# Local attention over six layers: the values product joins a ring of three PSUM banks, the output projection comes in two halves, and the slots are set anew

## The reference

```python
x = x + tanh(g_xattn) * xattn(layernorm(x), ctx)        # 4 x 512 x 128, once, small
h = layernorm(x)
for i in range(6):                                      # DEPTH
    s = shift_tokens(h)                                 # second half of the channels one token later
    q, k, v = split(s @ Wqkv[i])                        # 16 heads of 64
    q, k = l2norm(q) * q_scale[i], l2norm(k) * k_scale[i]
    q, k = rotary(q) * 8, rotary(k)
    # local attention: windows of 32 tokens see themselves and the window before
    p = softmax(mask(q @ k.T))
    h = (p @ v) @ Wo[i] + h
    s = shift_tokens(h)
    xn = (s - mean) / sqrt(var + 1e-5) * ln_g[i] + ln_b[i]
    a, gate = split(xn @ W1[i] + b1[i])                 # 341 each
    h = (a * gelu(gate)) @ W2[i] + b2[i] + h
x = x + tanh(g_ffn) * h
```

## Time and profile before

| | us |
|---|---|
| median of 3 runs (2105.93 to 2115.34) | 2112.6 |
| the profiled execution | 2110.48 |
| its span | 2108.7 |

### The profile page before, as it was taken

The page is one execution under the profiler, slowest core; times in us unless marked ns, Lnnn a source line. Parts: engine busy times, 40 slices in busy tenths (PEclk is TensorE's granted clock), DMA queues, the critical chain, the costliest instruction groups (busy, mean ns, idle before and its releaser), DMA issues.

```text
span 2108.7 us, 47754 instructions
## 1 busy us (share of the span) xinstructions
PE 1841.2 (87%) x17716; PEld 1082.4 (51%) x17716; DVE 1557.8 (74%) x2708; ACT 1314.2 (62%) x2363; POOL 1490.1 (71%) x1200
## 2 busy tenths in 40 slices
PE   6778888999899899889998888988898989989986
PEld 4445555555555555555555555555555555555542
DVE  4588778688678778687787776776877867867862
ACT  2366757657657657576576566575766765765762
POOL 2498678688677777786876776767868767868750
PEclk7699999999999999999999999999999999999998
DMA  3012212122222212222222221222222211221221
GB/s 94 20 52 69 60 50 61 47 59 68 56 59 68 54 49 72 58 64 55 52 57 58 70 63 51 59 53 60 69 53 60 63 49 50 53 61 49 56 54 30
DMA packets 154986, 120.41 MB, mean 57 GB/s; under 512 B 42577, under 2 KB 151173, under 8 KB 154629
## 3 DMA queue, kind: packets, MB, share of 16 engines
q1 hardware_dynamic: 154757, 117.35, 20.9%
HBM read 18.66 MB, written 1.05 MB: 9 GB/s over the span
## 4 chain that ended last, share of the span: by engine, by line
PE 40%; SPq 19%; DVE 18%; DMA 8%; ACT 7%; issue 6%; POOL 2%; DVEq 0%; POOLq 0%; ACTq 0%
SPq L1143 11%; PE ring_bank L456 8%; DMA vw<-vs 8%; PE sc_bank L408 5%; PE ring_bank L502 5%; SPq L1149 4%; PE qk_bank L363 4%; SPq L1146 4%; PE pv_bank L432 4%; PE ring_bank L421 3%; PE ring_bank L374 2%; PE ring_bank L395 2%; PE ring_bank L384 2%; PE ring_bank L445 2%; DVE xnT L921 2%
## 5 line engine op out<-in xcount | busy, mean ns | idle before, releaser
L1016 POOL TENSOR_TENSOR turned<-qkn,tables 128x512 f32<-128x512 f32 x384 | 489.5, 1275 | 462.7 <-DVE qkn L832 378.4
L1023 POOL TENSOR_TENSOR turned<-qkn,tables 128x512 f32<-128x512 f32 x384 | 489.8, 1276 | 0.0
L640 ACT ACTIVATE kB<-ring_bank 64x512 f32<-64x512 f32 x384 | 226.8, 591 | 335.3 <-PE ring_bank L395 333.1
L363 PE MATMUL qk_bank<-wqkv,xT 128*128 128x512 f32 x768 | 364.1, 597 | 0.0
L806 DVE TENSOR_REDUCE ss<-sq 128x16 f32<-128x1024 f32 x192 | 232.2, 1210 | 48.8 <-ACT sq L604 48.5
L878 DVE TENSOR_TENSOR o<-pv_bank,rr 128x512 f32<-128x512 f32 x192 | 132.1, 688 | 180.2 <-ACT oT L677 180.1
L1059 POOL TENSOR_TENSOR turned<-turned 128x512 f32<-128x512 f32 x192 | 251.2, 1308 | 15.1
L1052 POOL TENSOR_TENSOR turned<-turned 128x512 f32<-128x512 f32 x192 | 245.7, 1279 | 15.1
L613 ACT ACTIVATE vs<-ring_bank 128x512 f32<-128x512 f32 x192 | 114.3, 595 | 214.2 <-DMA vw<-vs 191.1
L408 PE MATMUL sc_bank<-kB,qT 128*32 128x128 f32 x6144 | 224.0, 290 | 2.8 <-ACT sc_bank L650 2.8
L604 ACT ACTIVATE sq<-qk_bank 128x1024 f32<-128x1024 f32 x192 | 196.3, 1023 | 42.7 <-PE qk_bank L363 39.6
(11 more groups left out here) (155 smaller groups left out, 3107.6 us busy)
## 6 DMA issues: line engine op xcount, KB each, us to landing
vw<-vs SPq DMA_DIRECT2D x1152, 64.0 KB, 2.0
vw<-vs SPq DMA_DIRECT2D x672, 32.0 KB, 1.9
wqkv<-in_L_ffn_Wqkv_dram SPq DMA_DIRECT2D x20, 384.0 KB, 3.3
wo<-in_L_ffn_Wo_dram SPq DMA_DIRECT2D x20, 128.0 KB, 3.2
w<-in_L_ffn_W_dram SPq DMA_DIRECT2D x6, 341.0 KB, 3.4
wqkv<-in_L_ffn_Wqkv_dram SPq DMA_DIRECT2D x1, 1536.0 KB, 9.8
x<-in_x_dram SPq DMA_DIRECT2D x2, 512.0 KB, 4.0
out_dram<-x SPq DMA_DIRECT2D x4, 256.0 KB, 2.3
```

What stands on the lines that cost most here:

```text
L363: mm = pe.matmul(QK[u % 2][:, i * UW:(i + 1) * UW], tok, wqkv[:, layer % 2, cut:cut + UW], start=True, stop=True)
L1016: return pool.tensor_tensor(heads(turned[:, u % 2, 2 * i, :]), heads(qkn[:, u % 2, i * UW:(i + 1) * UW]), table.unsqueeze(1).to_broadcast( ...
L1023: return pool.tensor_tensor(halves(turned[:, u % 2, 2 * i + 1, :]), halves(qkn[:, u % 2, i * UW:(i + 1) * UW])[:, :, ::-1, :], table.rearr ...
```

## The change

The bank of `attend` becomes the third bank of the ring. `attend` now takes a turn there, and every wait for `pv_mm` and `o_done` becomes one for its turn. `project_out` makes two products of 256 tokens, each after four units, and `add_attention` adds each half. DVE copies the variance with the epsilon added out of PSUM (`add_eps`), ACT's seed and the Newton step then read SBUF, and the square goes to `xnT`. The orders of all loops but POOL's are new: on PE `attend(n - 5)` comes right behind `queries_keys(n)`, then values, the transpose of o (one slot earlier than before), scores, the transposes of p and k (one slot later) and the transpose of q at the end; on DVE `newton` and `scale_k` work on unit n - 2 instead of n, the maxima on n - 4 instead of n - 2, and `scale_q(n - 2)` and `scale_o(n - 5)` come last; down and its addition come up to a slot 0 three groups behind. On SP `next_ffn`, the load of the next layer's W1, goes from slot 5 to slot 0, and `fold_bias`, which reads W1, from slot 6 to slot 0.

```diff
-SLOTS = UNITS + 14
+SLOTS = UNITS + 22
+RINGS = 3
+HALF = N // 2
...
-        PV_BANK = ctx.enter_context(nc.psum_tensor("pv_bank", [P, UW], F32))
-        RING = [ctx.enter_context(nc.psum_tensor(f"ring_bank{i}", [P, UW], F32)) for i in range(2)]
+        RING = [ctx.enter_context(nc.psum_tensor(f"ring_bank{i}", [P, UW], F32)) for i in range(RINGS)]
         ps = [QK[0][:, 0:UW], QK[0][:, UW:], QK[1][:, 0:UW], QK[1][:, UW:],
-              SC_BANK[:, :], PV_BANK[:, :], RING[0][:, :], RING[1][:, :]]
+              SC_BANK[:, :], RING[0][:, :], RING[1][:, :], RING[2][:, :]]
...
             def attend(u):
...
+                i = turn("pv", u)
                 pe.wait_ge(vw_dma[u % 2], vw_count(u))
-                pe.wait_ge(o_done, u)
+                pe.wait_ge(ring_read[i % RINGS], i // RINGS)
                 pe.wait_ge(*evicted("p", u))
                 for k in range(HP):
                     for w in range(NW):
...
                                        vw[:, u % 2, w, :, k * DH:(k + 1) * DH], start=True, stop=True,
                                        tile_position=(0, WIN * w))
...
+            def project_out(g, h):
...
-                i = turn("y", g)
-                pe.wait_ge(ring_read[i % 2], i // 2)
-                pe.wait_ge(*evicted("o", UPG * g + UPG - 1))
+                i = turn(f"y{h}", g)
+                pe.wait_ge(ring_read[i % RINGS], i // RINGS)
+                pe.wait_ge(*evicted("o", UPG * g + UPG // 2 * (h + 1) - 1))
                 for k in range(KO):
-                    mm = pe.matmul(RING[i % 2][:, :], wo[:, layer % 2, k, :], oT[:, k, :],
+                    mm = pe.matmul(RING[i % RINGS][:, 0:HALF], wo[:, layer % 2, k, :], oT[:, k, HALF * h:HALF * (h + 1)],
                                    start=(k == 0), stop=(k == KO - 1))
-                    if k == HP - 1:
-                        mm.then_inc(wo_half, 1)
-                mm.then_inc(ring_made[i % 2], 1)
...
-                if half == 0:
-                    act.wait_ge(wo_half, g)
-                elif g > 0:
-                    act.wait_ge(*evicted("y", g - 1))
...
+                if g > 0:
+                    act.wait_ge(*made(f"y{t // 2}", g - 1))
...
             def rstd_seed(g):
...
-                i = turns["var", g]
-                act.wait_ge(ring_made[i % 2], i // 2 + 1)
-                act.activation(rstd[:, :], RING[i % 2][:, :], ACT.Ln, bias=eps[:, 0:1]).then_inc(f_ln, 1)
+                act.wait_ge(*evicted("var", g))
+                act.activation(rstd[:, :], dsq[:, :], ACT.Ln).then_inc(f_ln, 1)
...
-                act.activation(dsq[:, :], rstd[:, :], ACT.Square, scale=0.5 ** 0.5).then_inc(f_half, 1)
+                act.activation(xnT[:, :], rstd[:, :], ACT.Square, scale=0.5 ** 0.5).then_inc(f_half, 1)
...
+            def add_attention(g, h):
...
+                i = turns[f"y{h}", g]
+                low, high = xT[0:64, g % B, HALF * h:HALF * (h + 1)], xT[64:C, g % B, HALF * h + 1:HALF * (h + 1) + 1]
+                dve.wait_ge(ring_made[i % RINGS], i // RINGS + 1)
+                dve.tensor_tensor(low, low, RING[i % RINGS][0:64, 0:HALF], ALU.add)
+                dve.tensor_tensor(high, high, RING[i % RINGS][64:C, 0:HALF], ALU.add).then_inc(ring_read[i % RINGS], 1)
...
+            def add_eps(g):
...
+                dve.wait_ge(ring_made[i % RINGS], i // RINGS + 1)
+                dve.tensor_scalar(dsq[:, :], RING[i % RINGS][:, :], LN_EPS, None,
+                                  ALU.add).then_inc(ring_read[i % RINGS], 1)
...
             def rstd_newton(g):
...
                 dve.wait_ge(f_half, g + 1)
-                dve.scalar_tensor_tensor(out=dsq[:, :], in0=RING[i % 2][:, :], scalar=eps[:, 0:1], in1=dsq[:, :],
-                                         op0=ALU.add, op1=ALU.mult).then_inc(ring_read[i % 2], 1)
-                dve.wait_ge(*evicted("var", g))
+                dve.tensor_tensor(dsq[:, :], dsq[:, :], xnT[:, :], ALU.mult).then_inc(f_newton, 1)
+                dve.wait_ge(f_newton, g + 1)
                 dve.scalar_tensor_tensor(out=rstd[:, :], in0=dsq[:, :], scalar=1.5, in1=rstd[:, :],
                                          op0=ALU.subtract, op1=ALU.mult).then_inc(rstd_done, 1)
...
             for n in range(SLOTS):
                 g, s = n // UPG, n % UPG
                 queries_keys(n)
+                attend(n - 5)
+                values(n)
+                transpose_o(n - 6)
+                scores(n - 3)
+                transpose_p(n - 4)
                 if s == 0:
+                    fold_bias(g - 2)
                     mean(g - 2)
-                if s == 2:
-                    up("a", 0, g - 2, 2)
-                values(n)
-                transpose_q(n - 2)
-                attend(n - 5)
+                if s == 3:
+                    up("gate", 1, g - 2, 0)
+                    up("gate", 1, g - 2, 2)
+                transpose_k(n - 2)
                 if s == 1:
-                    up("gate", 1, g - 2, 2)
-                    up("gate", 1, g - 2, 0)
-                    up("gate", 1, g - 2, 1)
-                transpose_o(n - 7)
-                transpose_p(n - 3)
-                scores(n - 2)
-                if s == 6:
-                    project_out(g - 1)
-                    fold_bias(g - 1)
-                if s == 4:
-                    down(g - 2)
-                transpose_k(n - 1)
-                if s == 0:
                     variance(g - 2)
                 if s == 2:
+                    project_out(g - 1, 0)
+                if s == 3:
+                    up("gate", 1, g - 2, 1)
+                    up("a", 0, g - 2, 0)
+                if s == 4:
+                    up("a", 0, g - 2, 2)
+                if s == 5:
                     up("a", 0, g - 2, 1)
-                if s == 3:
-                    up("a", 0, g - 2, 0)
-                if s == 5:
-                    transpose_out(g - 2)
+                if s == 6:
+                    project_out(g - 1, 1)
+                if s == 7:
+                    down(g - 2)
+                if s == 0:
+                    transpose_out(g - 3)
+                transpose_q(n - 2)
...
-            for n in range(-1, SLOTS):
+                act.wait_ge(ring_made[i % RINGS], i // RINGS + 1)
+                act.activation(uT[0:m, k, :], RING[i % RINGS][0:m, :], ACT.Gelu,
+                               bias=b1f[0:m, g // B % 2, 3 + k:4 + k]).then_inc(ring_read[i % RINGS], 1)
+
+            for n in range(SLOTS):
                 g, s = n // UPG, n % UPG
+                copy_qT(n - 3)
+                norm_seed(n - 1)
                 if s == 1:
+                    square_d(g - 2)
+                if s == 3:
+                    gelu_table(g - 2)
+                copy_v(n)
+                copy_oT(n - 6)
+                squares(n)
+                copy_pT(n - 4)
+                if s == 3:
                     gelu(g - 2, 0)
+                    gelu(g - 2, 2)
+                copy_kB(n - 2)
+                if s == 2:
+                    rstd_seed(g - 2)
+                if s == 3:
                     gelu(g - 2, 1)
-                copy_oT(n - 7)
-                if s == 1:
+                fill_mask(n - 2)
+                if s == 3:
                     exp_table(g - 2)
-                copy_pT(n - 3)
-                norm_seed(n)
-                copy_kB(n - 1)
-                if s == 0:
-                    rstd_seed(g - 2)
-                exponentials(n - 2)
-                squares(n + 1)
-                copy_v(n + 1)
-                if s == 7:
-                    square_d(g - 1)
-                if s == 0:
-                    gelu_table(g - 2)
-                copy_qT(n - 1)
-                if s == 0:
-                    gelu(g - 2, 2)
-                fill_mask(n - 1)
+                exponentials(n - 3)
...
             for n in range(SLOTS):
                 g, s = n // UPG, n % UPG
+                sum_p(n - 5)
+                newton(n - 2)
+                scale_k(n - 2)
+                maxima(n - 4)
+                invert_sum(n - 5)
+                less_maxima(n - 4)
+                if s == 1:
+                    add_bias(g - 2)
+                    centre(g - 2)
+                if s == 2:
+                    add_eps(g - 2)
+                if s == 5:
+                    gated(g - 2, 2)
+                if s == 6:
+                    gated(g - 2, 1)
+                sum_squares(n - 1)
+                if s == 0:
+                    add_ffn(g - 3)
+                clamp_squares(n - 1)
+                if s == 3:
+                    add_attention(g - 1, 0)
+                    rstd_newton(g - 2)
                 if s == 7:
-                    add_attention(g - 1)
-                    add_bias(g - 1)
+                    add_attention(g - 1, 1)
+                scale_q(n - 2)
+                scale_o(n - 5)
                 if s == 3:
-                    gated(g - 2, 1)
-                if s == 5:
-                    add_ffn(g - 2)
```

(28 more changed lines are left out.)

188 lines of the change are left out of this document (91 added, 97 removed).

## The result

The changed kernel takes 2394.8 us (2391.19 to 2397.98) beside 2113.2 us of the kernel before on the same chip: a ratio of 1.134, 95% interval 1.131 to 1.137. It is slower by 282 us.

What follows compares the result with a forecast made beforehand. DVE was taken to set the slot, in a cycle with PE; start 83.8 + slots 2256 (11.81 us each, clock falls included) + W1 47 + drain 83 + 2 = 2472, rounded to 2465 us; range 2290 to 2620.

Steps and rivals of the forecast that it cites:

- The cycle: DVE and PE, each slot: scale_q releases QK, PV follows, scale_o waits for PV; 9.5 us without feed-forward work.
- The slots without the clock: Slots s0 to s7 with DVE's feed-forward work at full clock: 88.5 us a group, 11.06 a slot.
- clock-free sum: Whole kernel with no falls of the clock: 2326 us, 2328 with time around the span; as a rival, 27%.
- Held operations: DVE's clamp held until POOL's current operation ends: 0.5 us a slot, ends 0 and 1.1.
- The clock: PE's idle gaps bring four clock falls a group, 1.5 us each: slot 11.81 us instead of 11.06.
- W1: SP's next_ffn behind ten copies in slot 0 delays fold_bias and DVE's centre: 9.5 us, five times, 47 us.
- The halves: Output projection in two halves: same PE work, 3.5 us per half; DVE's four pieces instead of two add 0.1 us.
- The drain and the start: Time after the last and before the first queries and keys: drain 83 us, start unchanged at 83.8 us.
- The ring: Values' third bank removes the stall of 191.1 us waiting for copies, but gains nothing, because DVE is late next.
- The variance in SBUF: DVE's Newton square with two SBUF operands might be held by POOL, some 30 us in all; put at nothing.
- The second rival: Short cycle: nothing held, PE on time, clock kept; slot 10.0 us, 2080 us in all; chance 6%.

Runs made afterwards that it cites:

- exchanging the two lines: On the changed kernel, attend(n-5) placed ahead of queries_keys(n) on PE instead of behind it: 2059.3 us, ratio 0.975.
- one line in the old ring: On the kernel before, attend(n-5) alone moved on PE to directly behind queries_keys(n), two banks kept: 2011.6 us, ratio 0.950.
- the kernel before with the cycle put in: On the kernel before, attend(n-5) directly behind queries_keys(n), scale_o(n-4) directly behind scale_q(n-1), dependent steps shifted: 3286.7 us, ratio 1.556.
- its repaired form: On the changed kernel, attend(n-5) ahead of queries_keys(n) on PE and the next W1 load in slot 7 on SP: 2025.7 us, ratio 0.958.

## Why the prediction was right, and where it was off

Forecast 2465, measured 2394.8: slower, by the mechanism named, and 70 us too much. By its steps:

- **The cycle.** Right. scale_o starts 3.2 us after scale_q's end (put at 3.0), DVE's largest wait is scale_o for the product, 687 us (500 or more said), PE's is queries and keys for scale_q, and exchanging the two lines removes it. PE is busy for 79% of the span, where some 75% was said.
- **The slots without the clock.** By slot, s0 to s7, the forecast was 10.1, 10.5, 12.8, 10.1, 11.9, 10.3, 11.3, 11.5, 88.5 in all. With the gaps filled in all slots but slot 4 the medians are 10.50, 10.44, 13.08, 9.79, 12.22, 10.43, 11.63, 11.86: 89.95. The time of that run, 2341.5, stands against 2328 for the clock-free sum. No slot is off by more than 0.4 us.
- **Held operations.** 0.5 us a slot was too much. The clamp's mean is 297 ns and the Newton product's 192, against 174 without holding: 0.14 us in all. The rest of the cycle came out: DVE's steps from the start of scale_o to the end of scale_q take 5.9 us by their starts (1020.90 to 1026.04, then 0.09 for the clamp and 0.69; 6.0 put), with 3.2 ahead of them 9.1 us, against 9.5. Slots that a late product of PE sets (s2, s6) never had the term. With 0.36 us less in the others the forecast would have been 86.3 to 87.1 us a group, as six or four slots contain it, so products and steps were put some 0.4 us a slot too early (in s2 the addition of the output half starts at 10.07, put at 9.9, and takes 0.88, put at 0.7), and the two errors cancel. That is luck.
- **The clock: the term that failed.** I took four falls a group at 1.5 us, 137 us in all. The kernel after has about two a group, and filling the gaps gives 53 us back. The price of one was right (slot 5 12.06 against 10.43, 1.6 us), and so were six gaps a group (126 of 2 us and more between 200 and 2200 us); the share of them with a fall was not. In the kernel before a fall begins in or right behind 15 of 21 such gaps up to 2000 us, the two in three of the prediction, but in the kernel after behind 43 of 126: slot 5 has 22 in 22 groups, slot 3 nine, slot 0 eight (five of them the long ones at the late W1), slot 2 three, slot 1 one, the others none.
- **W1.** 47 us forecast, 43.6 on the chip, by 8.38 us of waiting in the row above against 9.5.
- **The halves.** Right at nothing: 3.62 us each, against 7.13 for one whole.
- **The drain and the start.** 76.4 and 86.0, against 83 and 83.8.
- **The ring.** The prediction said that the third bank takes the stall of the earlier trace rows away and that DVE is late next. In the kernel after the stall is gone. But the same ring in the old slots keeps it, and one line in the old ring nearly removes it, so it was the order. This claim was wrong in its cause; the number didn't hang on it.
- **The variance in SBUF.** add_eps, the square and the last step take 691 to 693 ns each; the square is not held in any of 24 cases. Put at nothing, and so it is, as POOL is idle there.
- **The second rival.** Its sum, 83.8 + 1910 + 83, leaves out the 47 us of W1. With them its 10.0 us a slot gives 2126 us, no longer faster than before, so the case that was to be the faster one wasn't. The forecast didn't use it.

With the clock term at 53 and the rest as it stood, the sum is 2328 + 53 = 2381, 14 us under the result.

## What to carry to other kernels

Ask of each wait which release it hangs on, and follow that through all queues back to the waiting engine: if the way closes within one slot, the two engines take turns, however low their busy shares are; a step between the two gives slack only if nothing behind it needs the same slot's work. A bank more in the ring took no stall away here, because the same change added a turn: count the turns between a slow reader and the one that needs its bank. Before spending a bank on a stall, try moving what frees its source earlier; here that one line was worth more than all of the change.

## What was not expected of the hardware

- **Falls of the clock are shared between gaps, not tied to one.** Gaps of 2.1 to 2.9 us, and five longer ones at the late W1, came in most slots of the kernel after and the clock fell after one in three; filling the gap ahead of slot 5 moved 22 falls of 22 to slot 6. In the kernel before with the cycle put in, where such gaps last 2.9 to 7.2 us, it fell after all 121 between 200 and 2200 us, eight a group. The Trainium skill, "TensorE: Matmul & The Clock Gate", "HAM oscillation", tells of a loop with a DMA wait of some 3 to 5 us in each iteration that starts every iteration cold. The run with the long gaps agrees, though its waits are for other engines; the kernel after has shorter gaps, of which that section doesn't tell, and two falls a group.
- **Idle of one engine can turn into busy time of another.** The same 128x16 product on DVE lasts 174 ns in the median where POOL is idle and 1195 where POOL works. The normalization of 128x512 lasts 743 ns in the kernel after and 1445 in the exchanged one, where it begins 0.37 us after an instruction of POOL in 22 of 24 cases; in the other two POOL is idle and it takes 741 and 752 ns. The rows of the latter kernel, then of the kernel after:

```profile
L930 DVE SCALAR_TENSOR_TENSOR xnT<-dT,cols,rstd x24: 741/1445/1450, 251.1 to 2039.0; 128x512 f32<-128x512 f32 x24
```

```profile
L930 DVE SCALAR_TENSOR_TENSOR xnT<-dT,cols,rstd x24: 740/743/751, 273.8 to 2373.8; 128x512 f32<-128x512 f32 x24
```

The Trainium skill, "SBUF — State Buffer", "Who interferes with whom", says that a DVE instruction with two SBUF inputs contends with a GpSimd instruction that reads SBUF, and that the later of the two is blocked until the other has finished. Both instructions of DVE here have two inputs in SBUF, and the trace agrees in the main: all 22 and all 163 long cases begin inside an instruction of POOL. It isn't the whole account, for in the kernel after 13 of the 24 normalizations begin in the last 0.2 us of an instruction of POOL and still take 743 ns. The exchanged kernel pays for its tighter slots with 1608 us of busy DVE in its repaired form, against 1382, and is still faster by 369 us.
